# Squares one unit ahead, the roots in another rhythm, and block two's rows loaded ahead of the contexts, in a three-layer decoder kernel

## Time and profile before

| | before |
|---|---|
| runs without the profiler, us | 1863.18, 1865.43, 1866.70 (median 1865.43) |
| the profiled execution, us | 1867.18 |
| its span, first to last instruction, us | 1865.5 |
| PE busy | 1325.9 (71%) |
| DVE busy | 1254.0 (67%) |
| POOL busy | 1000.8 (54%) |
| ACT busy | 849.6 (46%) |
| mean DMA rate over the span | 64 GB/s |

### The profile page before, as it was taken

How to read it: one execution, slowest core, us unless ns; L and a number is a source line. 1 busy time by engine, 2 the same in 40 slices (tenths; PEclk the granted TensorE clock), 3 DMA queues, 4 the chain that set the end, 5 groups by cost and what they waited for, 6 DMA issues and landing times. The chain is left out here.

```text
span 1865.5 us, 32852 instructions
## 1 busy us (share of the span) xinstructions
PE 1325.9 (71%) x9000; PEld 1151.7 (62%) x9001; DVE 1254.0 (67%) x3301; ACT 849.6 (46%) x2808; POOL 1000.8 (54%) x1234
## 2 busy tenths in 40 slices
PE   6277106850036676766765899998489999999997
PEld 4265105630025465654654778876389999999997
DVE  3798999999988999999876144454434444443442
ACT  5433213442113665667766488887322322322332
POOL 3367868987669999998866324342111122122121
PEclk9689558885568878878877999998789999999999
DMA  5344001566031010100002111133130410411200
GB/s 139 74 102 111 12 6 42 143 173 95 23 120 38 23 33 18 32 27 27 28 27 84 57 42 52 54 120 120 40 103 21 154 48 22 158 42 45 77 17 7
DMA packets 182719, 119.29 MB, mean 64 GB/s; under 512 B 124849, under 2 KB 163560, under 8 KB 182120
## 3 DMA queue, kind: packets, MB, share of 16 engines
q1 hardware_dynamic: 119848, 90.98, 17.4%
q10 hardware_dynamic: 58864, 18.71, 4.0%
q0 software_dynamic: 3920, 8.60, 1.3%
HBM read 83.44 MB, written 35.74 MB: 64 GB/s over the span
## 5 line engine op out<-in xcount | busy, mean ns | idle before, releaser
L246 POOL TENSOR_TENSOR wt<-wt 128x1024 f32<-128x1024 f32 x128 | 301.5, 2355 | 53.9 <-DVE wt L191 46.9
L252 POOL TENSOR_TENSOR wt<-wt 128x512 f32<-128x512 f32 (+2 forms) x384 | 307.6, 801 | 30.1
L1942 PE MATMUL e_ph<-e_g,e_w 128*128 128x128 f32 x2496 | 285.2, 275 | 0.7 <-ACT e_g L1912 0.7
L1942 PEld LDWEIGHTS e_ph<-e_g,e_w 128*128 128x128 f32 x2496 | 281.9, 192 | 0.9 <-issue 0.9
L191 DVE SCALAR_TENSOR_TENSOR wt<-wt,scan 128x256 f32<-128x256 f32 x512 | 242.0, 473 | 18.0 <-POOL wt L246 13.4
L170 DVE TENSOR_REDUCE wt<-wt 128x16 f32<-128x272 f32 x512 | 219.2, 428 | 0.1
L181 DVE TENSOR_TENSOR scan<-wt,scan 128x256 f32<-128x256 f32 x512 | 215.0, 420 | 0.3
L159 DVE TENSOR_TENSOR wt<-wt,scan 128x256 f32<-128x256 f32 x512 | 210.1, 410 | 0.9 <-PEq L269 0.5
L1420 ACT ACTIVATE wt<-p_pX,p_mx 128x120 f32<-128x120 f32 x512 | 176.4, 387 | 71.9 <-DVE p_mx L1205 70.3
L1903 ACT ACTIVATE e_g<-e_ph,wt 128x128 f32<-128x128 f32 x156 | 48.7, 363 | 304.9 <-PE e_ph L1942 304.9
L1821 POOL TENSOR_TENSOR e_ve<-e_mv,eps 128x1 f32<-128x1 f32 x39 | 7.4, 190 | 327.1 <-DVE e_mv L1877 327.1
(11 more groups left out here) (226 smaller groups left out, 2925.0 us busy)
## 6 DMA issues: line engine op xcount, KB each, us to landing
wt<-in_L_ffn_W SPq DMA_DIRECT2D x24, 1024.0 KB
qkv<-f_st ACTq DMA_DIRECT2D x48, 256.0 KB, 2.6
p_kE<-kE SPq DMA_DIRECT2D x16, 480.0 KB, 3.7
p_vP<-vP SPq DMA_DIRECT2D x16, 480.0 KB
wt<-qkv SPq DMA_DIRECT2D x12, 512.0 KB, 6.4
e_xt<-routed ACTq DMA_DIRECT2D x39, 130.0 KB, 2.1
f_xt<-in_x SPq DMA_DIRECT2D x32, 128.0 KB, 2.8
p_oT<-o SPq DMA_DIRECT2D x16, 256.0 KB
```

The costliest lines, as they stand in the source:

```text
L246: nc.gpsimd.tensor_tensor(x, s["S"][:, h, z * Q:(z + 1) * Q], s["qn"][:, h, z * Q:(z + 1) * Q].rearrange("p t (o d) -> p t o d", o=1).to_b ...
L252: nc.gpsimd.tensor_tensor(x[:, :, :, 0:half], x[:, :, :, 0:half], x[:, :, :, half:2 * half], ALU.add).then_inc(s["o_fold"][h], 1)
L1942: ins = nc.tensor.matmul(ph2[:, c // 2, c % 2], w2[:, s, i, c * P:(c + 1) * P], g1[:, i], start=(i == 0), stop=(i == C1 - 1))
```

## The change

1. **Squares one unit ahead.** ACT does the squares of unit n+1 in step n, behind the scaling of unit n (`squares_of`), into a PSUM tensor `squared`; `xt`, `ss`, `ms` and `rstd` have three slots (`XS = 3`), and `load_rows` runs three units ahead.
2. **Roots in another rhythm.** On POOL the ring's `sem_inc`s come right after the front's first seven steps; no inverse root stands ahead of the first group. Units 4 to 9 stand behind groups 0 to 5, unit 10 behind group 7, units 11 to 15 behind groups 14 to 18. POOL's chunks 0 to 9 are written out; 10 to 15 are a loop. ACT does its side of part 1's lengths after step 10, not 12.
3. **Block two's raw rows first.** The four `load_raw` calls for parts 2 and 3 stand behind the loads of `wk` and `wv` and ahead of the contexts. The contexts' buffer `ct` lies over `acc`.
4. **Gates in DRAM in the scan's order.** The tensor `gates` has the sequence pair ahead of the group of heads. A unit's gates are stored with eight DMAs of 4 KB (four of 8 KB before), and a half part is loaded with one DMA of 32 KB per gate (four of 8 KB each before): two L379 DMAs per call in place of eight.

```diff
+XS = 3
@@ front_and_scan
-        ct, cT = sb("ct", [CTX, 2, D]), sb("cT", [P, 2, G, CTX])
+        ct, cT = shaped(acc[0:CTX].rearrange("c g b t -> c (g b t)"), (2, D)), sb("cT", [P, 2, G, CTX])
+        squared = ps("squared", [P, 2, D])
+        MEASURE = 5
@@ store_gates
-                    eng.dma_start(k["gates"][i, n, g].rearrange("a q h t -> h (a q) t"),
-                                  bst[32 * i + g * H // G:32 * i + (g + 1) * H // G]).then_inc(gates_out[n >= U], 16)
+                    for a in range(2):
+                        eng.dma_start(k["gates"][i, n, a, g].rearrange("q h t -> h q t"),
+                                      bst[32 * i + g * H // G:32 * i + (g + 1) * H // G, 2 * a:2 * a + 2]).then_inc(gates_out[n >= U], 16)
@@ load_rows
-                if n >= 2:
-                    sp.wait_ge(xn_done, (n - 1) * 2)
+                if n >= XS:
+                    sp.wait_ge(xn_done, (n - XS + 1) * 2)
@@ load_raw
                         for y in range(2):
-                            for pair in range(U):
-                                sp.dma_start(s["gate"][32 * pair:32 * pair + 32, jb, h, 1 + y, now],
-                                             k["gates"][y, rows.start + pair // 2, :, pair % 2].rearrange("g q h t -> g (q h) t")).then_inc(gate_in[h], 16)
+                            sp.dma_start(s["gate"][:, jb, h, 1 + y, now], k["gates"][y, rows].rearrange("u a g q h t -> (u a g q h) t")).then_inc(gate_in[h], 16)
@@ sync, behind the loads of wk and wv
+            for h in range(2):
+                for part in (2, 3):
+                    load_raw(part, h)
...
             pipeline(sp, NB, 3, contexts)
-            for h in range(2):
-                for part in (2, 3):
-                    load_raw(part, h)
@@ gpsimd
             for step in range(U + 3):
                 if step < U:
-                    inverse_rms((step, step % 2, step // 2))
+                    inverse_rms(step, step % XS)
                 if step >= 3:
                     store_gates(pool, step - 3)
-            for n in range(U, U + 2):
-                inverse_rms((n, n % 2, n // 2))
...
+            for c in range(3):
+                chunk(c, {z: (U + c * 2 + z, U + c * 2 + z) for z in range(2)})
+            chunk(3, {1: (NU - 6, NU - 6)})
+            for c in range(MEASURE - 1, MEASURE + 2):
+                chunk(c)
+            chunk(MEASURE + 2, {0: (NU - 5, NU - 5), 1: (NU - 4, NU - 4)})
+            ready(1)
+            chunk(MEASURE + 3, {0: (NU - 3, NU - 3), 1: (NU - 2, NU - 2)})
+            chunk(MEASURE + 4, {0: (NU - 1, NU - 1)})
+            with pool.Fori(MEASURE + 5, CHUNKS) as c:
+                chunk(c)
@@ scalar
+            def squares_of(n):
+
+                act.wait_ge(x_in[n % XS], n // XS * 32 + 32)
+                if n >= 1:
+                    act.wait_ge(rstd_done, n * 2)
+                for q in range(2):
+                    nc.scalar.activation(squared[:, q], xt[:, n % XS, q], ACT.Square, accum_out=ss[:, n % XS, q:q + 1]).then_inc(ss_done, 1)
...
                 if a is not None and a >= U:
                     n, slot = a, a % 2
                     act.wait_ge(rstd_done, n * 2 + 2)
+                    act.wait_ge(T_done, n - 1)
...
+                if a is not None and a + 1 < (U if a < U else NU):
+                    squares_of(a + 1)
...
-            units(U, NU, {2 * U + 4: (*lengths(1, 0), *lengths(1, 1))})
+            units(U, NU, {2 * U + 2: (*lengths(1, 0), *lengths(1, 1))})
```

More of the change, by code:

```diff
@@ L275, in front_and_scan @@
         cw, cb = sb("cw", [P, G, KC]), sb("cb", [P, G])
-        xt = sb("xt", [P, 2, 2, D])
-        ss, ms, rstd = (sb(n, [P, 2, 2]) for n in ("ss", "ms", "rstd"))
+        xt = sb("xt", [P, XS, 2, D])
+        ss, ms, rstd = (sb(n, [P, XS, 2]) for n in ("ss", "ms", "rstd"))
         xn = sb("xn", [P, 2, 2, D])
@@ L312, in front_and_scan @@
         BIT, ODD, EVEN, NORM1, BIAS_K = 1, 2, 3, 4, 4 + G
-        x_in, ct_in, kv_out = ([sem(f"f_{n}{i}") for i in range(2)] for n in ("x_in", "ct_in", "kv_out"))
+        x_in = [sem(f"f_x_in{i}") for i in range(XS)]
+        ct_in, kv_out = ([sem(f"f_{n}{i}") for i in range(2)] for n in ("ct_in", "kv_out"))
         out = [sem(f"f_out_{n}") for n in "qkv"]
@@ L347, in load_rows @@
             def load_rows(n):
-                part, u, s = n // U, n % U, n % 2
-                if n >= 2:
-                    sp.wait_ge(xn_done, (n - 1) * 2)
+                part, u, s = n // U, n % U, n % XS
+                if n >= XS:
+                    sp.wait_ge(xn_done, (n - XS + 1) * 2)
                 for q in range(2):
@@ L375, in load_raw @@
                         later = part > 0
-                        sp.wait_ge(gates_out[later], 64 * (units - U * later))
+                        sp.wait_ge(gates_out[later], 128 * (units - U * later))
                         for y in range(2):
-                            for pair in range(U):
-                                sp.dma_start(s["gate"][32 * pair:32 * pair + 32, jb, h, 1 + y, now],
-                                             k["gates"][y, rows.start + pair // 2, :, pair % 2].rearrange("g q h t -> g (q h) t")).then_inc(gate_in[h], 16)
+                            sp.dma_start(s["gate"][:, jb, h, 1 + y, now], k["gates"][y, rows].rearrange("u a g q h t -> (u a g q h) t")).then_inc(gate_in[h], 16)
                     else:
@@ L475, in _, with chunk @@
             ready(0)
-            half = CHUNKS // 2
-            with pool.Fori(0, half - 5) as c:
+            def chunk(c, units={}):
                 for z in range(R // Q):
                     outputs(c, z)
[L480 to L495, removed]
+                    if z in units:
+                        n, slot = units[z]
+                        inverse_rms(n, slot % XS)
+            for c in range(3):
[9 more added lines that the diff above has]
+                chunk(c)
         @block.vector
@@ L627, in _ @@
             act.wait_ge(set_up, SETUPS)
-            def step(a, b, c):
[L631 to L638, removed]
+            def squares_of(n):
[4 more added lines that the diff above has]
+                    nc.scalar.activation(squared[:, q], xt[:, n % XS, q], ACT.Square, accum_out=ss[:, n % XS, q:q + 1]).then_inc(ss_done, 1)
+            def step(a, b, c):
                 if c is not None:
@@ L643, in step @@
                     act.wait_ge(rstd_done, n * 2 + 2)
+                    act.wait_ge(T_done, n - 1)
                     for q in range(2):
-                        nc.scalar.activation(xn[:, slot, q], xt[:, slot, q], ACT.Copy, scale=rstd[:, slot, q:q + 1]).then_inc(xn_done, 1)
+                        nc.scalar.activation(xn[:, slot, q], xt[:, n % XS, q], ACT.Copy, scale=rstd[:, n % XS, q:q + 1]).then_inc(xn_done, 1)
+                if a is not None and a + 1 < (U if a < U else NU):
+                    squares_of(a + 1)
                 if b is not None:
@@ L724, in units @@
             def units(first, last, between):
+                squares_of(first)
                 for at in range(first, last + 2):
@@ L1977, in build @@
         "qkv": nc.dram_tensor("qkv", (3, NU, 2, G, 2, P, PT), F32, kind="Internal").ap(),
-        "gates": nc.dram_tensor("gates", (2, NU, G, 2, 2, H // G, PT), F32, kind="Internal").ap(),
+        "gates": nc.dram_tensor("gates", (2, NU, 2, G, 2, H // G, PT), F32, kind="Internal").ap(),
         "o": nc.dram_tensor("o", (JB, NB // 2, G, 2, P, TB), F32, kind="Internal").ap(),
```

20 lines of the change are left out of this document (9 added, 11 removed).

## The result

Timed in three rounds, the changed kernel took 1881.76 us (median of six runs, 1876.84 to 1883.92) against 1867.13 for the kernel before: a ratio of 1.0074, 95% interval 1.0058 to 1.009, **14.6 us slower**. Timed again, on another chip, it took 1876.24 against 1864.80: 1.0053, interval 1.0036 to 1.007, 11.4 us slower. The forecast was 8.3 us slower, with 1879 as its upper end; it counted from 1865.43 us, the median of three runs, where the median of six is 1867.13.

The account below looks back on a forecast made before the run. DVE was taken to bound the first stage, whose shift passes to the end. Waits -16.1, head +1.9 and late square +22.5 sum to +8.3 us: 1865.43 becomes 1873.7, range 1857 to 1879 (8 in 10).

Parts of the forecast that it names:

- I let a shift of DVE in the first stage pass to the end one for one.: First stage, the scan's: DVE sets its length, so any shift there reaches the kernel's end in full.
- The 16.1 us of waits for POOL: Scan up to chunk 13: DVE's waits of 4.5 and 11.6 us go; gain 16.1, bounds 10 and 16.1.
- The head: Ahead of the scan: more gate DMAs on POOL start the scan 1.9 us later; bounds 1.5 earlier, 4 later.
- Part 1's first square: ACT's moved step 10: square done at 183.7 to 186.2, wanted at 187.6; nothing taken, bounds 0 and 3 us later.
- The rows of the next unit are a step ahead: ACT's squares in the front: the next unit's rows are there a step early, so third slots cost nothing.
- When the units end: Front's last units on ACT: unit 15 scaled at 328.9 against 317.58, 11.3 us later, not counting the head's 1.9.
- The raw loads: Block two: twelve of 512 KB at 220 GB/s, 28 us together, ahead of the first context, which lands at 383.4.
- The first rival: Block two's raw loads hold up nothing much: first context at 371, sum -8, 1857 us; chance 0.22.
- Contexts and wait: Block two: contexts take 60.5 us, k's square is done at 445.8, wanted by DVE in chunk 14 at 423.3.
- The term of +22.5: Chunk 14: k's square comes 22.5 us after DVE wants it, a wait of that size.

Follow-up runs that it names:

- first pair: The first profiles of the kernel before and of the changed kernel, both unedited: spans 1865.5 and 1879.8 us.
- second pair: Both kernels profiled once more on the same chip, no edit: the kernel before 1866.26 us, the changed one 1876.24.
- the runs with six and twelve ahead: Six: changed kernel with only half 0 of block two's raw rows ahead of the contexts, 1860.48 us; twelve: changed kernel itself, 1876.24.

## Why the prediction was wrong

The direction and the mechanism in the front were right, the size was not: 8.3 us forecast, 14.6 and 11.4 measured, and the first of these lies 2.8 us above the range, 1.7 of them by the base (1867.13 for 1865.43).

- **"I let a shift of DVE in the first stage pass to the end one for one."** This is the step that failed. Up to block two the first pair of profiles shows +7.7 us and the second +10.0 (503.38 to 513.39), against a forecast of +8.3. Behind it, where the forecast had nothing, the changed kernel takes 4.0 and 3.1 us more when profiles with the same stretch are compared; why is open. On top of that the stage has two lengths 4.4 us apart, with either kernel; the range took no account of it, nor of which of them the forecast's own base, one profile with the short one, had.
- **The 16.1 us of waits for POOL.** They went, all of them. But the kernel before has that much of them only in its first profile; its second has 13.2, so that the gain was sized by one profile. DVE gained more in part 1's sums: 4.5 us in the first pair. The first went from 4.77 us, with POOL busy for 4.43, to 2.72 behind DVE's wait for ACT; the second from 4.16, here before, with POOL busy for 3.84, to 1.72 beside an idle POOL:

```profile
211.41 4.16 DVE L559 TENSOR_TENSOR wt<-wt 128x512 f32<-128x512 f32 x4
```

```profile
198.64 1.72 DVE L559 TENSOR_TENSOR wt<-wt 128x512 f32<-128x512 f32 x4
```

I had not priced that. In the second pair it is 2.7 us (4.76 to 4.48, 4.17 to 1.72).
- **The head.** Forecast 1.9 us later, measured 2.99 and, in the second pair, 3.24. Eight DMAs take POOL 4.44 us, as taken (4.3), but those of unit 1 land 4.0 us behind the last issue and not 2.8. `bst` is filled the last time at 49.33 us, 5.1 us later than in the earlier trace rows, where I had 3.8:

```profile
32.99 4.44 POOL L347 DMA_DIRECT2D gates<-f_bst  x8 [2.83 <-ACT f_bst L693]
...
42.08 4.44 POOL L347 DMA_DIRECT2D gates<-f_bst  x8 [4.65 <-ACT f_bst L693]
```

- **Part 1's first square.** Bounded by 0 and 3 us, taken as 0: 2.97 in one profile, none in the other, 6.31 in the run with the raw rows behind. The square comes at 191.95 and 190.31 where 186.7 to 189.2 was forecast, with the head's 3 us. "The rows of the next unit are a step ahead" did not hold: ACT stood 9.29 and 8.29 us for those of unit 11, which SP loads behind part 1's raw rows.
- **When the units end.** 328.9 + 1.9 = 330.8 forecast, 332.24 measured. The last steps take 13.26 us (forecast 13.3), the first after the pause 16.5 (14.9), the second 14.75. That 13.3 fits is luck: the terms given for it, 13.0 - 0.8 - 1.0 + 1.35, add up to 12.6. The run with the old gates shows what goes out, 1.2 us and not 1.8 (13.03 to 11.87).
- **The raw loads.** From the first issue to the first context 37.1 us forecast (the terms for the last raw row add up to 383.8 us, not the 383 given), 38.4 measured. The fit that the prediction quotes from the Trainium skill (DMA: Bandwidth & Descriptors, Anatomy of one DMA) is given there for DMAs issued from GpSimd; these are issued from SP, and the runs with six and twelve ahead show 2.3 to 2.4 us for each, as the rows said. The first rival, that they hold up nothing much, would have needed it below 25.
- **Contexts and wait.** 60.5 us forecast, 60.4 measured. The wait is 26.16 us for 22.5, and 3.0 of it come back, since the sum behind it runs alone. The term of +22.5 is so 23.2 net, 23.3 in the second pair. Together: 3.0 - 16.1 - 4.5 + 3.0 + 23.2 = 8.6 for the 7.7 us of the first pair, 3.2 - 13.2 - 2.7 + 23.3 = 10.6 for the 10.0 of the second.

One reason that I gave for the units' late end is put differently by the runs: it is the rhythm of the roots (unit 15 is scaled at 303.06 us, 29 earlier, in the run with early roots), but the doubled gate stores too. Without them unit 15 comes 12.6 us earlier, 3.4 of them by the head; I had 1.35 us a step, and it is 1.39 in the last two steps but 2.5 and 2.9 in the two after the pause.

## What to carry to other kernels

A transfer moved ahead of other work is free only if what stands behind it on the same queue is not late itself: before moving it, add the queue's own drain time to the start of the next item and compare with the moment its last reader wants it. When a change takes waits out of the engine that bounds a stage, list every hand-over to that engine later in the stage with its slack in microseconds; here the slack was 16.6 us, the bound moved 15.5 us earlier and the supplier 27 later. And a base of one profile carries the base's own luck: profile the unchanged kernel twice before a range is drawn, and compare profiles in which the untouched part has the same length.

## What the runs showed of the hardware that I had not expected

- The same five rounds of block two's stage take 277.1 us (seven profiles, the longest 277.5) or 281.5 us (six), and nothing between, whatever was changed in the front. In the long ones POOL is busy 258.1 to 258.3 us instead of 254.7 to 255.1 and DVE 275.5 to 275.7 instead of 272.7 to 273.9; the granted clock is 0.82 in all four lines above. What picks one is open.
- DVE's four sums over rows of up to 1024 elements take 5.71 us while POOL works on the scan's states (busy for 5.3 of them, in the kernel before and in the run with early roots), and 2.74 us when POOL has run dry (busy for 0, in the changed kernel after DVE's wait). A wait of DVE so costs less than its length here. That this is one engine's access to SBUF slowing the other's was not measured by itself.
- Squares of 128x256 written to PSUM take 0.37 us (median of 24), to SBUF 0.41 (median of 24 before; the one in the earlier trace rows took 0.42).
